# Copying the turned q and k of two token groups out of PSUM on VectorE instead of ScalarE

## The reference

```
x_norm = layernorm(layernorm(x)) * ln_w + ln_b
q = l2norm(split_heads(x_norm @ Wq))          # 16 heads of 8
k = l2norm(split_heads(x_norm @ Wk))
v = split_heads(layernorm(x) @ Wv)
align = einsum('bhtd,bhsd->bhts', q, k)
resonance = sigmoid((align - THRESH) * SHARP)
modulation = resonance * gate_q[..., :, None] * gate_k[..., None, :]
attn = einsum('bhts,bhsd->bhtd', modulation, v) @ Wo + bo
x = x + layernorm(attn)
# then: router, the two best of 8 experts for each token, a shared expert, layernorm, residual
```

## Time and profile before

| | |
|---|---|
| median of 3 runs | 727.62 us (724.76, 727.62, 728.91) |
| profiled execution | 728.29 us, of it 726.5 us from the first to the last instruction (the span) |
| mean granted TensorE clock | 0.94 of full |
| PE / ACT / DVE busy | 617.6 / 565.6 / 419.7 us |
| prologue | from the start to the last copy of turn 3 at about 79 us |

### The profile page before, as it was taken

How to read it: one execution, slowest core, us unless ns; L and a number is a source line. 1 busy time by engine, 2 the same in 40 slices (tenths; PEclk the granted TensorE clock), 3 DMA queues, 4 the chain that set the end, 5 groups by cost and what they waited for, 6 DMA issues and landing times.

```text
span 726.5 us, 15317 instructions
## 1 busy us (share of the span) xinstructions
PE 617.6 (85%) x5928; PEld 259.6 (36%) x5928; DVE 419.7 (58%) x1105; ACT 565.6 (78%) x663; POOL 163.4 (22%) x149
## 2 busy tenths in 40 slices
PE   3577999999999999999999999989999993475840
PEld 2453211112222344432334444323344441465840
DVE  6775184930552545538635865475458546665975
ACT  1578799999999999989899999888989991033510
POOL 1122000000032122200525212024441210245732
PEclk9999999999999999999999999999999997577975
DMA  8600001630034344410534445105434440293721
GB/s 325 230 30 30 30 9 19 259 111 1 9 107 139 112 132 145 136 51 2 176 116 143 146 130 141 33 22 173 138 113 136 142 131 1 71 333 135 229 79 51
DMA packets 47639, 82.02 MB, mean 113 GB/s; under 512 B 5456, under 2 KB 25168, under 8 KB 47568
## 3 DMA queue, kind: packets, MB, share of 16 engines
q1 hardware_dynamic: 45088, 76.31, 32.8%
q0 software_dynamic: 2048, 4.20, 2.1%
q10 hardware_dynamic: 432, 0.54, 0.3%
HBM read 64.59 MB, written 16.45 MB: 112 GB/s over the span
## 4 chain that ended last, share of the span: by engine, by line
PE 70%; DVE 13%; issue 5%; ACT 3%; DMA 3%; POOL 2%; SPq 1%; POOLq 0%; DVEq 0%
PE AV L876 36%; PE GB L950 14%; PE S L862 7%; PE UO L862 3%; PE GB L897 2%; ACT res L746 1%; DVE work L1381 1%; DVE gate_q L1540 1%; DVE coll L1257 1%; DVE work L1374 1%; PE GB L945 1%; POOL xs_dram L624 1%; DMA gu_ring<-gu_dram 1%; PE UO L842 1%; DVE work L1516 1%
## 5 line engine op out<-in xcount | busy, mean ns | idle before, releaser
L746 ACT ACTIVATE res<-S 128x1024 f32<-128x1024 f32 x348 | 348.8, 1063 | 22.8 <-PE S L862 11.2
L876 PE MATMUL AV<-res,vg 128*8 128x512 f32 x2048 | 305.2, 599 | 1.9 <-DVE coll L1257 1.8
L746 ACT ACTIVATE res<-UO 128x1024 f32<-128x1024 f32 x164 | 174.7, 1065 | 8.5 <-PE S L862 7.2
L650 POOL TENSOR_TENSOR work<-work 128x512 f32<-128x512 f32 x64 | 82.5, 1289 | 290.7 <-DVE work L1381 286.6
L862 PE MATMUL S<-qT,kT 32*128 32x512 f16 x696 | 104.3, 388 | 2.3 <-ACT res L746 2.1
L950 PE MATMUL GB<-xT,gu_ring 128*128 128x128 f16 x1128 | 81.7, 224 | 12.9 <-DVE place L1356 6.0
L721 ACT ACTIVATE work<-work,scl 128x512 f32<-128x512 f32 x64 | 46.7, 730 | 43.5 <-DVE work L1374 43.5
L1374 DVE TENSOR_SCALAR work<-GB,scl 128x512 f32<-128x512 f32 x56 | 45.3, 810 | 59.9 <-PE GB L950 59.3
L862 PEld LDWEIGHTS S<-qT,kT 32*128 32x128 f16 x696 | 25.7, 91 | 145.7 <-ACT res L746 93.5
L950 PEld LDWEIGHTS GB<-xT,gu_ring 128*128 128x128 f16 x1128 | 65.4, 100 | 34.0 <-issue 17.6
L624 POOL DMA_INDIRECT xs_dram<-xrow,slot x32 | 31.7, 990 | 185.4 <-DVE slot L1361 177.1
(11 more groups left out here) (252 smaller groups left out, 681.0 us busy)
## 6 DMA issues: line engine op xcount, KB each, us to landing
gu_ring<-gu_dram SPq DMA_DIRECT2D x54, 512.0 KB, 3.5
dn_ring<-dn_dram SPq DMA_DIRECT2D x56, 256.0 KB, 2.9
work<-in_gu SPq DMA_DIRECT2D x8, 512.0 KB, 10.5
gu_dram<-gu_ring SPq DMA_DIRECT2D x8, 512.0 KB, 2.7
ys_dram<-work SPq DMA_DIRECT2D x60, 64.0 KB, 2.7
work<-in_down SPq DMA_DIRECT2D x8, 256.0 KB, 10.9
dn_dram<-dn_ring SPq DMA_DIRECT2D x8, 256.0 KB, 2.9
kT<-gu_dram SPq DMA_DIRECT2D x4, 512.0 KB, 7.4
```

Source lines behind the costliest of these rows:

```text
L650: nc.gpsimd.tensor_tensor(hid[u % 2], prod[u % 2], sg[u % 2], ALU.mult).then_inc(hid_ready, 1)
L746: nc.scalar.activation(res[:, k % 2, 2 * half:2 * half + 2, :].rearrange("p h t -> p (h t)"), score_banks(i, k, half).rearrange("p h t -> ...
L876: mm = nc.tensor.matmul(AV[32 * j:32 * j + HD, :], vg[:, s, G * g + j, :], res[:, k % 2, j, :], start=s == 0, stop=s == ST - 1)
```

## The change

The four copies of turn 1 and of turn 2 leave ACT's program and go into DVE's, as `tensor_copy` where they were `activation(Copy)`. ACT keeps those of turn 0; DVE keeps those of turn 3. On DVE turn 1 stands behind `unit(2)` and `gated_values(2)` and ahead of `low_parts(2)`; turn 2 stands behind `unit(3)` and `gated_values(3)` and ahead of `low_parts(3)`. The wait for the stored q (q_saved), which guards `q_out` before it is overwritten, moves along.

```
@@ ACT
             def turn(b):
                 for n in range(4):
-                    if n == 0 and b >= 2:
-                        act.wait_ge(q_saved, b * 16)
                     act.wait_ge(qk_tr, b * 4 + n + 1)
                     nc.scalar.activation(*turned_bank(b, n), ACT.Copy).then_inc(qk_copied, 1)
...
-                    if (what, b) == ("turn", NB - 1):
+                    if what == "turn" and b > 0:
                         continue
@@ DVE
+            def turn(b):
+                if b >= 2:
+                    dve.wait_ge(q_saved, b * 16)
+                for n in range(4):
+                    dve.wait_ge(qk_tr, b * 4 + n + 1)
+                    v.tensor_copy(*turned_bank(b, n)).then_inc(qk_copied, 1)
             for b in range(NB):
                 unit(b)
                 gated_values(b)
+                if b >= 2:
+                    turn(b - 1)
                 low_parts(b)
             gate_weights()
-            dve.wait_ge(q_saved, (NB - 1) * 16)
-            for n in range(4):
-                dve.wait_ge(qk_tr, (NB - 1) * 4 + n + 1)
-                v.tensor_copy(*turned_bank(NB - 1, n)).then_inc(qk_copied, 1)
+            turn(NB - 1)
```

## The result

The changed kernel takes 740.68 us (median; 738.51 to 741.06, 4 runs) against 726.19 for the kernel before (724.05 to 728.91). The ratio is 1.0191, with a 95% interval from 1.0147 to 1.0236: slower by 10.7 to 17.1 us.

What follows compares the result with a forecast made beforehand. No engine was taken as full from 30 to 84 us; the chain of waits through the q copies bounds it. 6.08 + 6.23 + 1.40 = 13.7 us on the median 727.62 gives 741.3 us, range 737.0 to 746.8.

Steps and rivals of the forecast that it cites:

- ACT's 7.94 us are worth nothing: Eight copies leaving ACT free 7.94 us of busy time there; credited with nothing, as it becomes idle time.
- The rival in which they come off the time: ACT's work sets the prologue's pace, so 7.94 us come off, giving 720.4 us; chance 0.03.
- Turn 1, 6.08 us: Copies wait on DVE behind gated_values(2) until 52.14; PE goes on at 55.02 instead of 48.94, 6.08 us late.
- Turn 2, 6.23 us: Copies wait behind gated_values(3) until 73.51; scores of round 3 come 12.31 us late, 6.23 of it from turn 2.
- The cost of the copy: Each q copy on DVE takes 0.65 us, against 0.96 to 1.07 on ACT; a whole turn takes 2.78 us.
- The store that turn 2 has to wait for: Second store of q, issued about 53.4, lands in 2.6 us, before 73.5; no cost unless over 17 us.
- The clock, 1.40 us: PE's idle waits put the second pairs of transposes in turns 1 and 2 at half clock: 1.40 us, bounds 0 to 1.40.
- Nothing is given back: After 84 us PE and ACT are too full to recover the 13.7 us; rival of no change, 727.6 us, chance 0.03.
- The place in the order, not the engine: On DVE the copies stand behind unit and gated_values of the next group, though banks are ready when that stretch begins.

Runs made afterwards that it cites:

- fillers: Products with unused results, run on PE during its waits; added to the kernel before they gave 724.97 us, to the whole change 735.59 us.
- the half: Only turn 1's copies moved to DVE in the kernel before, with unused products filling PE's waits: 730.63 us, ratio 1.0067.
- turn 1 alone: Kernel before with only turn 1's copies moved to DVE, turn 2's left on ACT: 735.18 us, ratio 1.0121.
- ACT's wait: Kernel before, copies of turns 1 and 2 still on ACT but waiting there for gated_values of the next group: 743.54 us, ratio 1.0238.
- turn 2 alone: Kernel before with only turn 2's copies moved to DVE, turn 1's left on ACT: 732.72 us, ratio 1.0085.
- the kernel before with fillers: Kernel before plus short unused products on PE in turns 1 and 2 and rounds 3 to 6: 724.97 us, ratio 0.997.

## Why the prediction was right

**ACT's 7.94 us are worth nothing**: right for this pair. ACT's busy time fell by 7.4 us and its idle stretches grew to 11.52 and 10.15. The rival in which they come off the time fell with the result. That ACT was busy for 41.50 of 54 us there said nothing of what its time is worth. With fillers a little of it is worth something: the sigmoids of round 3 start 1.02 us behind the scores where ACT's copies of k still run, and 0.42 behind them where both turns are on DVE, so 0.60 us come back.

**Turn 1, 6.08 us**: right in place and size. The copies started at 51.93 (52.14 was forecast, from a trace whose squares came 0.13 us later), and with the clock held high the half costs 5.97.

**Turn 2, 6.23 us**: the mechanism is right. At the scores of round 3 both waits together make 30.08 - 17.76 = 12.32 us at the high clock (from the squares, with fillers), where 12.31 was forecast. At the first gate turn 2 costs 5.73, less by the 0.60 that come back behind the scores.

**The cost of the copy**: 0.65 us each was forecast, and the pairs took 1.28. Whether work on POOL would add to it is not shown: POOL was idle while DVE copied (its first instructions behind the two turns start at 59.66 and 82.13). The store that turn 2 has to wait for left DVE no idle time at 73.95; the bound given for it, 17 us, was a slip, since from 53.4 to 73.5 there are 20.

**The clock, 1.40 us**: right in size, with some luck. In this pair of executions the step holds as it was written: the second pairs took 1.86 us each (1.92 forecast), and what follows was slow before as well as after (the products took 1.89 us at 50.41 and 1.90 at 57.02). The kernel before loses 2.90 us of its prologue to the low clock (49.30 - 46.40) and the change 4.68 (62.80 - 58.12); the difference, 1.78, is the term at the first gate. At the scores of round 3 it is 13.53 - 12.32 = 1.21. The luck is in the base: that the stretch behind turn 1 is slow was taken from one execution, and three others with the same program up to turn 2 did not have it (13.16 and 13.17 us to turn 2, not 14.26). Had the profiled execution been like these, the difference would have been some 1.1 us larger, by this estimate 2.9. The rule of the Trainium skill ("TensorE: Matmul & The Clock Gate", HAM oscillation) that a long enough wait ends at the half clock is borne out by the fillers, which take the loss away without taking the wait away: the second pairs took 1.86 us behind the bare waits and 1.29 behind the filled ones. The drop of the kernel before at 49 us is another matter, since PE's longest wait in the 10 us ahead of it was 1.18 us.

**Nothing is given back**: right for the attention, 13.37 us at the first gate and 12.98 at the last. The rest behind the last gate stays open, as said above; the medians of the times differ by 14.5.

**The place in the order, not the engine**: the argument of the whole forecast. It was shown from both sides: the wait alone, put on ACT, costs 14.78 us at the first gate, and the copies on DVE ahead of `unit` cost 1.08.

One thing stays open. Most ratios stand for somewhat more than the way to the first gate says: for turn 1 alone 8.8 us (5.6 to 12.1) against 5.82, for ACT's wait 17.3 (14.5 to 20.1) against 14.78. Both intervals still hold the smaller number. The profiled execution of the kernel before, 728.29 us, lies 1.6 us above the median of its runs (726.7 in the last comparison), and its slow stretch behind turn 1 accounts for 1.1 us of the way that the three executions alike up to there do not have. That this is the whole of it is not shown; the prologue of other executions of the kernel before was not profiled.

## What to carry to other kernels

A copy that releases a bank belongs where its engine is free when the bank is ready. Before it is moved to an idler or faster engine, look for what stands ahead of it in that engine's order: here a chain of 7 us of small instructions, which started at the very moment the bank was full, and the turn's advantage of about 1 us (3.75 us of ACT's copies against 2.78) was lost six times over. Put ahead of that chain, for turn 2, the same copy was worth something, once the next consumer of the chain got room too: 1.56 us of the way at an even clock.

Costs that are read from one profiled execution each need a base whose clock is the same in all of them. Here they missed 3.9 us, and the medians of the times did not. Where the granted clock has two levels in the stretch, hold it high in every version, or read the clock beside each difference, and see whether the medians show the same gap.

## What the hardware showed that had not been expected

Kernels whose programs are alike up to turn 2 fell to the low clock at the same place in one execution and not in others. From 44 to 49 us the kernel before and the version with turn 2 alone issue the same work, PE busy for 2.35 and 2.28 of 5 us; then the clock was 0.51 from 49 to 52 us in the one and 1.00 in the other (above). The two versions with turn 2 on DVE ahead of `unit(3)`, alike up to there as well, also had 1.00 (2.28 and 2.52 of 5 us). So the low clock is not fixed by the program alone. What decides is not shown: from 40 to 44 us PE was busy for 2.84 us in the kernel before and for 3.69 to 4.00 in the other three. With more work on PE in the waits (4.18 of 5 us there in the kernel before with fillers) the clock was 1.00 from 44 to 92 us in all four kernels of the table with fillers; unused products made the kernel before faster by 2.2 us (1.0 to 3.3).
